# Layer 3's cross attention placed earlier behind each sequence, with its last exponentials in two PSUM banks

## What is computed

```
# L3 self attention: 16 heads of width 64, softmax over keys, then Wo
# L3 cross attention, over heads inside each token:
q = (query @ Wq.T + bq).reshape(N, L, 16, 8)      # query = layernorm(x)
k = (key @ Wk.T + bk).reshape(N, L, 16, 8)        # key = value = context
v = (value @ Wv.T + bv).reshape(N, L, 16, 8)
energy = einsum('nlhd,nlgd->nlhg', q, k)          # 16 x 16 per token
attn = softmax(energy / sqrt(128), axis=g)
out = einsum('nlhg,nlgd->nlhd', attn, v).reshape(N, L, 128)
out = (out - mean) / sqrt(var + eps) * ln_g + ln_b
x = x + out @ Wo.T + bo
```

## Time and profile before

| | us |
|---|---|
| median of 3 runs | 1126.06 |
| runs | 1125.48, 1126.06, 1141.29 |
| the profiled execution's own time | 1124.19 |
| its span, first to last instruction | 1122.3 |
| last addition of the cross attention begins | 990.05 |
| first instruction of the block behind the barrier | 992.71 |

### The profile page before, as it was taken

How to read it: one execution, slowest core, us unless ns; L and a number is a source line. 1 busy time by engine, 2 the same in 40 slices (tenths; PEclk the granted TensorE clock), 3 DMA queues, 4 the chain that set the end, 5 groups by cost and what they waited for, 6 DMA issues and landing times. The chain is left out here.

```text
span 1122.3 us, 15955 instructions
## 1 busy us (share of the span) xinstructions
PE 822.0 (73%) x5961; PEld 597.9 (53%) x5969; DVE 611.0 (54%) x1414; ACT 349.2 (31%) x683; POOL 316.3 (28%) x318
## 2 busy tenths in 40 slices
PE   4974896974657185579887764999999896257994
PEld 2542453573434073367754432677877686135984
DVE  2644862313299952486565787855335337942221
ACT  1110475330112111125544560454343232111331
POOL 1344100203148724122221111000034045615222
PEclk9985798895678677689998895999999998568998
DMA  9302200450000004325365000000000000005674
GB/s 370 135 2 84 70 5 1 126 166 18 20 0 1 0 1 92 87 52 119 72 165 158 4 1 1 1 2 1 1 2 1 1 1 1 0 1 198 216 265 141
DMA packets 44678, 72.44 MB, mean 65 GB/s; under 512 B 4817, under 2 KB 36737, under 8 KB 43033
## 3 DMA queue, kind: packets, MB, share of 16 engines
q1 hardware_dynamic: 38921, 65.72, 19.7%
q0 software_dynamic: 1728, 3.59, 0.9%
q10 hardware_dynamic: 3952, 2.10, 0.7%
HBM read 58.65 MB, written 15.89 MB: 66 GB/s over the span
## 5 line engine op out<-in xcount | busy, mean ns | idle before, releaser
L847 DVE TENSOR_REDUCE space<-PS 128x2 f32<-128x512 f32 x128 | 83.2, 686 | 40.1 <-PE PS L651 39.9
L2545 DVE TENSOR_REDUCE space<-PS 128x2 f32<-128x512 f32 x64 | 43.3, 689 | 80.5 <-PE PS L2242 80.3
L831 ACT ACTIVATE annex<-PS 128x384 f32<-128x384 f32 (+1 forms) x128 | 67.2, 544 | 58.2 <-PE PS L662 29.1
L2261 PE MATMUL PS<-space 64*128 64x256 f32 x256 | 68.0, 411 | 4.6 <-issue 4.6
L2281 PEld LDWEIGHTS PS<-space 128*128 128x128 f32 x512 | 61.7, 193 | 17.4 <-issue 16.5
L2281 PE MATMUL PS<-space 128*128 128x65 f32 x512 | 69.1, 282 | 0.2 <-ACT space L2363 0.2
L1950 POOL TENSOR_TENSOR space<-space 128x1536 f32<-128x1536 f32 x16 | 54.6, 3437 | 38.3 <-DVE space L1881 32.1
L1170 PE MATMUL PS<-space 128*128 128x128 f32 x444 | 57.1, 284 | 7.9 <-DVE space L1305 5.0
L2242 PE MATMUL PS<-space 64*128 64x256 f32 x256 | 62.7, 401 | 0.1
L1305 DVE TENSOR_TENSOR space<-PS,space 128x512 f32<-128x512 f32 (+1 forms) x28 | 19.2, 687 | 75.8 <-ACT space L1232 70.6
L1170 PEld LDWEIGHTS PS<-space 128*128 128x128 f32 x444 | 53.3, 197 | 10.9 <-DVE space L1305 6.0
(11 more groups left out here) (492 smaller groups left out, 2209.9 us busy)
## 6 DMA issues: line engine op xcount, KB each, us to landing
space<-in_e_l_ffn SPq DMA_DIRECT2D x22, 768.0 KB, 5.3
space<-in_e_l_ffn SPq DMA_DIRECT2D x23, 192.0 KB, 3.0
l_ffn_sorted<-in_slots SPq DMA_DIRECT2D x2, 1584.0 KB, 25.6
space<-l_attn_scratch_k SPq DMA_DIRECT2D x8, 384.0 KB
space<-l_ffn_sorted SPq DMA_DIRECT2D x10, 264.0 KB, 4.4
weights<-in_w_l_xattn SPq DMA_DIRECT2D x1, 2504.0 KB, 15.2
weights<-in_w_l_attn SPq DMA_DIRECT2D x1, 2124.0 KB, 11.9
space<-l_xattn_scratch_q SPq DMA_DIRECT2D x4, 512.0 KB, 3.5
```

The lines of the kernel that those rows point to most:

```text
L831: nc.scalar.activation(P[:, u % 8, 0:keys], PS[:, 3 + u % 2, 0:keys], ACT.Exp).then_inc(exp_done, 1)
L847: nc.vector.tensor_reduce(m[:, :, at_h], max_bank(u).rearrange("p (c k) -> p c k", c=2), AX_X, ALU.max).then_inc(max_done, 1)
L2261: nc.tensor.matmul(out, kk[:, 128 * kc:128 * kc + 128], q, start=True, stop=False)
L2545: nc.vector.tensor_reduce(MX[:, b % 2, :, h], PS[:, max_bank[a], :].rearrange("p (c k) -> p c k", c=2), AX_X, ALU.max).then_inc(max_done, 1)
```

## The change

All of it is in `feedforward_attentions`.

1. The six jobs t, t, o, t, t, o of a sequence's self attention output stood in six steps, 4 to 9 after the sequence's last second scores (4, 5, 6, 8, 9, 10). They now stand in four: 3, 3, 4, 4, 5, 6.
2. A sequence's cross attention begins (`first_x`) in the step of its last `o`, not one later. `xk` and `xv` stand two and one steps before that, not on it and one after. With 1, `first_x` is 34, 50, 64 and 72, where it was 39, 55, 69 and 77.
3. The pieces from `products` on stand closer together. For sequences 2 and 3 they have a list of their own, and `products` stands in the step of `xq`. `xw` of sequence 2 is placed five steps behind its `xo`.
4. The second scores keep to banks 3 and 4 for all units; from unit 43 on they took banks 0, 1, 3 and 4. TensorE's wait at unit 43 for all maxima is gone, and ScalarE waits for all maxima before it writes sequence 2's values and queries into banks 1 and 0.

No instruction is added or removed; the pipeline has 86 steps from step 0 on instead of 97.

```diff
@@ -2038,7 +2038,7 @@
         if u % 2:
             norms[second_at(u) + 2].append(u // 2)
     max_bank = [(0, 1, 3, 4)[a % 4] if a < HEADS else a % 2 for a in range(UNITS)]
-    exp_bank = [3 + i % 2 if i < ALONE else (0, 1, 3, 4)[(i - ALONE) % 4] for i in range(UNITS)]
+    exp_bank = [3 + i % 2 for i in range(UNITS)]
     user_before = lambda banks, u: max((x for x in range(u) if banks[x] == banks[u]), default=None)
     count, job_at, piece_at = collections.defaultdict(int), {}, collections.defaultdict(list)
 
@@ -2058,8 +2058,8 @@
     for b in range(B):
         place(first_at(16 * b + 15) + 3, "M", b, 0)
         for i in range(6):
-            place(second_at(16 * b + 15) + 4 + i + i // 3, ("t", "t", "o")[i % 3], b, i)
-    first_x = [job_at["o", b, 5] + 1 for b in range(B)]
+            place(second_at(16 * b + 15) + (3, 3, 4, 4, 5, 6)[i], ("t", "t", "o")[i % 3], b, i)
+    first_x = [job_at["o", b, 5] for b in range(B)]
     f = place(PLAN["f1"][0], "w", 0, 0)
     piece(f + 1, "weights", 0)
     place(-20, "b", 0, 0)
@@ -2081,21 +2081,23 @@
             place(second_at(16 * b) - 6 + i, "v", b, i)
         f = first_x[b]
         piece(f, "cross", b)
-        place(f, "xk", b, 0)
-        place(f + 1, "xv", b, 0)
+        place(f - 2, "xk", b, 0)
+        place(f - 1, "xv", b, 0)
         piece(f + 1, "normedx", b)
         f = place(f + 2, "xT", b, 0)
         f = place(f + 1, "xq", b, 0)
-        for i, what in ((1, "products"), (3, "sum0"), (5, "sum1"), (5, "shift"), (6, "expx"), (7, "dens"), (7, "values"),
-                        (9, "weigh0"), (12, "weigh1"), (12, "scale"), (13, "out"), (14, "normedo")):
-            if b in SHARED and what[:-1] in ("sum", "weigh"):
-                continue
-            piece(f + i, what, b)
-            if b in SHARED and what in ("products", "values"):
-                piece(f + i, "sum1" if what == "products" else "weigh1", b)
-                piece(f + i, "sum0" if what == "products" else "weigh0", b)
-        f = place(f + 15, "xo", b, 0)
-        place(f + 1, "xw", b, 0)
+        if b in SHARED:
+            for i, what in ((0, "products"), (0, "sum1"), (0, "sum0"), (2, "shift"), (3, "expx"), (4, "dens"), (4, "values"),
+                            (4, "weigh1"), (4, "weigh0"), (6, "scale"), (7, "out"), (8, "normedo")):
+                piece(f + i, what, b)
+            f = place(f + 9, "xo", b, 0)
+            place(f + (5 if b < B - 1 else 1), "xw", b, 0)
+        else:
+            for i, what in ((1, "products"), (3, "sum0"), (4, "sum1"), (4, "shift"), (5, "expx"), (6, "dens"), (6, "values"),
+                            (8, "weigh0"), (9, "weigh1"), (9, "scale"), (10, "out"), (11, "normedo")):
+                piece(f + i, what, b)
+            f = place(f + 12, "xo", b, 0)
+            place(f + 1, "xw", b, 0)
     jobs = sorted((step,) + job for job, step in job_at.items())
     number = {j[1:]: i for i, j in enumerate(jobs)}
     FROM, TO = PLAN["in"][0], jobs[-1][0] + 1
@@ -2250,8 +2252,6 @@
                     pe.wait_ge(max_placed, 16 * 6 * (i // HEADS + 1))
                 if i == 0:
                     pe.wait_ge(max_done, HEADS)
-                if i == ALONE:
-                    pe.wait_ge(max_done, UNITS)
                 if earlier is not None:
                     pe.wait_ge(exp_done, earlier + 1)
             for kc in range(2):
@@ -2337,6 +2337,7 @@
                     act.wait_ge(multiplied, products_before(b - 1) - 2)
                 dst = {"xk": KX, "xv": VX, "xq": QX}[kind][:, b % 2]
                 if b in SHARED and kind != "xk":
+                    act.wait_ge(max_done, UNITS)
                     nc.scalar.copy(PS[:, SHARED[b] + (kind != "xq"), 0:128], out[:, 128:256]).then_inc(beside, 1)
                 ins = nc.scalar.copy(dst, out[:, 0:256].rearrange("p (t d) -> p t d", t=2))
             ins.then_inc(free[bank_of[i]], 1)
```

## The result

The changed kernel took 1137.55 us, the median of 6 runs (1131.64 to 1144.19), against 1127.97 for the kernel before beside it (6 runs, 1125.48 to 1141.29). The ratio is 1.0095, 95% interval 1.0054 to 1.0136. The forecast was 1127.4, with a range up to 1133.0: the time lies above it.

A forecast was written before the change was run, and what follows sets the result against it. Inside one pipeline ending at a barrier, TensorE's work bounds first, then VectorE's order; sequence 3's `products` 1.7 us later less 0.35 gave +1.3, so 1126.06 + 1.3 = 1127.4 us, range 1121.5 to 1133.0.

The forecast's parts named there:

- Part 3: Steps 58 to 67: added jobs lengthen 36.2 us to 42.0; `products` of sequence 2 starts 9.1 us earlier.
- Part 4: From sequence 2's `products` to the end: VectorE's order and low clock use up the 9.1 us; end at 991.8, +1.3.
- my clock rival: Work at the end runs at full clock instead of partly at half: 1123.8 us; chance 0.2.
- Part 1: TensorE's ledger, steps 31 to 57: jobs moved ahead of step 56 add 3.6 us, waits for VectorE 1.2.
- the upper bound: Steps 31 to 57: sequence 1's `t` waits at most one VectorE reduction, 2.28 us, ahead of its normalise.
- Part 2: Step 58's stall: the 6.0 us from last maxima's transposes to next scores stay; scores resume 2.6 us later.
- port block: VectorE's normalisation of sequence 1's result, 4.74 us behind GpSimd's product instead of about 0.6, goes from before sequence 2's `products`.
- The banks cost nothing: Two exponential banks cost nothing given 0.75 us of cover; the rival had 4 us, 1131.4 in all, chance 0.1.
- The full clock at the end: Rival: the last transposes, `o` and projections run at full clock, 1123.8 us; chance 0.2.
- The moved port block: Rival: GpSimd wins the port at sequence 3's `products`, VectorE waits 4.46 us, 3.6 more, 1131.0; chance 0.1.
- The held maxima: Rival: VectorE's reductions in steps 40 to 47 hold up the maxima; later chains move by up to 9; chance 0.05.

The follow-up runs named there:

- filled_long: Changed kernel with 25 matmuls of constants, never read, behind the transposes of the last maxima, filling TensorE's stall; ratio 0.9984.
- before_filled: Kernel before with 25 never-read matmuls in the stall and nothing else; gained 1.0 us in the record, nothing that the times show.
- packed_banks: Kernel before with the outputs' transposes and projections packed, exponentials in two banks, and `first_x` in the step of the last `o`; time not given.
- banks_alone: Kernel before with only the fourth edit's bank line: second scores of the last 21 units keep to banks 3 and 4; ratio 1.0002.
- norm_first: Changed kernel with sequence 2's `products` and both sums one step later, behind the last normalise on VectorE; ratio 0.9998.
- late_both_banks: before_late_both with the exponentials of all steps in two banks too; 268.0 us from the first M to the last addition.
- before_late_both: Kernel before with sequence 0's `xw` and sequence 1's `xq` both moved behind step 61's first `t`; 268.0 us from first M to last addition.
- tail_order: norm_first plus sequence 3's statistics and normalisation ahead of sequence 2's `values` and weighs, and sequence 2's layer normalisation later; ratio 1.0030.

## Why the prediction was wrong

**The step that failed** is Part 3: "893.6 to 929.84 is 36.2 ... 42.0". The ledger of jobs came near. With the clock held (`filled_long`), the stretch takes 39.8, 2.2 less than forecast. Of these, 1.6 are low clock that the 36.2 of before already held: `before_filled`, without it, takes 34.6 (898.13 to 932.75). But the ledger's price of a job was that of full clock, taken from a stretch of before with TensorE busy and the clock at 1.00, and nothing in the part says what keeps the clock there. The changed kernel took 50.9 us: 11.1 more than at the full clock, and 8.9 more than forecast, out of 11.4 by which the whole was off. I had looked for low clock in Part 4 only, and my clock rival went the other way, to less of it. The sign of the risk was in the profile: the first score matmuls behind the stall took 1.18 us for four, against 0.71 a few steps later.

The Trainium skill (TensorE: Matmul & The Clock Gate, What's actually happening) says that activity releases the throttle. This trace doesn't bear that out as it stands: TensorE was busy for 7.00 of 7.00 us from 903 to 910 at a granted clock of 0.50, and the clock rose only at 925.5. The measurement decides.

**The step that was mis-sized** is Part 1's sum. The last M came 3.95 us later relative to the first, against 2.6. `packed_banks` has 3.97 and `banks_alone` 0.00, so the packing costs it. Of the 1.35 over, TensorE's waits for VectorE explain 0.8; the rest is open. In steps 31 to 57 there is 1.17 behind an addition of layer 2's feed-forward part, 0.62 behind a normalise and four of 0.26 behind additions, 2.8 in all, against 1.4 before, a rise of 1.4; net of the wait for `xT` that went, I had 0.6. These rows of the changed kernel's timeline are the main ones:

```profile
795.04 1.09 PE L2196 MATMUL PS<-const_tile,annex 128*128 128x128 f32 x8 [1.17 <-DVE X L2532]
...
854.17 1.07 PE L2196 MATMUL PS<-const_tile,annex 128*128 128x128 f32 x8 [0.62 <-DVE annex L2566]
```

None is a reduction's 2.28, the upper bound. The wait of 1.17 is for a line (L2532) that the prediction didn't name.

**Right in the working:**
- Part 2's 6.0 us of stall stood in every kernel, with `xw`, without it, and with 12 or 25 matmuls in it; only `before_filled`, with both in it, took 6.6. What the idle time was filled with changed the clock, not the resumption.
- Part 3's port block went (0.60 for 4.74), and `products` stood at the last weighted values.
- Part 4's order held line by line, `expx` behind the third `t` included. I had 30.0 between the two `products`, and it was 30.8. The `o` took 4.05 with its last two matmuls, where I had 3.2, but `expx` came only 0.3 late. The other 0.5 stands behind `weigh0`, where the normalisation took 0.90 beside a GpSimd instruction of 0.63 that had begun 0.06 ahead (978.31 and 978.37). I had 24.3 to the end, and it was 24.4. `norm_first` shows that the 7.3 us idle ahead of the last normalise is the price of standing `products` in front of it.
- The banks cost nothing. From the resumption to the last weighted values no second scores of the changed kernel wait for ScalarE; `banks_alone` has a ratio of 1.0002, and `late_both_banks` against `before_late_both` has the same 44.6 and 268.0.
- Relative to the first M, `filled_long` has sequence 2's `products` at 212.0 (forecast 212.7), sequence 3's at 243.2 (242.7), the end at 267.5 (267.0). The terms behind these cancel in part: +1.35 for the last M, -2.2 for the stretch behind the resumption, +1.2 between the two `products`.

**The rivals.** The full clock at the end did not come in the changed kernel; `norm_first` got it for the `t` and the `o` by its edit. The moved port block did not come in the changed kernel: GpSimd started its product only behind VectorE's (983.34 against 983.00). In `tail_order` it came at another place, with 5 us. The held maxima showed as the 1.35 at most, not 9. None of my cases had TensorE at the low clock for over 20 us while it is busy.

## What to carry to other kernels

A stretch in which an engine is 100% busy has a price per job only as long as its clock is what it was. Where a change empties or reorders TensorE's work around an idle time, both clocks belong in the range, and a cheap experiment tells them apart: fill the idle time with matmuls that nobody reads, and look whether the stretch behind shrinks. And a piece moved to where its data is ready can stand in front of one that another engine waits for; here that cost 7 us on TensorE and one step in the table gave 6 of them back. A reordering that shortens one wait can also put a VectorE normalisation right behind the start of a GpSimd product; in `tail_order` that cost 5 us.

## What the runs showed of the hardware that I had not expected

- In nine records TensorE's clock stayed at 0.50 for 13.7 to 27.3 us in and behind an idle time of 4.6 to 5.7 us. For all but the first 2.9 to 4.3 us of that the engine was busy without a gap, with the same instructions that elsewhere ran at 1.00. In five records with idle times of the same size it was 3.4 to 10.2 us.
- Twelve matmuls of 128x512 in the stall (2.76 us, 3.01 idle left) left 10.2 us of it; twenty-five (5.57 us, 0.21 idle left) left none, in five records of five.
- VectorE's normalisation of 0.60 us took 5.65 (`tail_order`) when it began 0.06 behind a GpSimd product of 5.37, and 0.90 when it began 0.06 behind a GpSimd instruction of 0.63.
- The distance from the first M to the last addition repeats within 0.6 us between two profiles of one kernel (278.4 and 277.8, 269.2 and 269.2, 260.9 and 260.9), while the runs of one kernel spread over 4 to 21 us. For a change inside one block it is the finer scale, but it is that of one execution; `norm_first` at 272.1 and 0.9998 beside `tail_order` at 269.2 and 1.0030 shows that the order of the ratios doesn't always agree.
